# A graph layer's products of messages, each as two products on the two column halves of TensorE's array

## What is computed

```python
h  = silu(edge_scalars @ Wfc1 / 4)                 # per edge
w  = h @ Wfc2 / 8                                  # w0, w1, w2, w3
e0, e1 = f0[edge_src], f1[edge_src]                # gathered, turned features
mid0 = w0 * e0 * sh0;  mid1 = w3 * (e1 . sh1) / sqrt(3)
mid2 = w1 * e0 * sh1;  mid3 = w2 * e1 * sh0
n0..n3 = mean of mid0..mid3 over the edges of a destination node
alpha  = [n0, n1] @ Wa
conv   = [[n0, n1] @ Wl2_s, [n2, n3] @ Wl2_v]
out    = layernorm(x + sc + alpha * conv)
```

## Time and profile before

| | before |
|---|---|
| median of 3 timed runs | 932.54 us (929.51 to 934.15) |
| span of the profiled execution, first to last instruction | 930.5 us |
| TensorE busy | 880.9 us (95%) |
| VectorE busy | 812.1 us (87%) |
| GpSimd busy | 714.5 us (77%) |
| ScalarE busy | 632.5 us (68%) |
| products y on TensorE, L733 and L736 | 141.6 and 182.3 us |

### The profile page before, as it was taken

One profiled execution on the slowest core, in us unless ns is written; L12 is line 12 of the kernel. 1 busy time (PEld: TensorE's weight loads), 2 busy tenths in 40 slices (PEclk: granted clock), 3 DMA queues, 4 the chain that ended last, 5 costly groups with the idle time before them and its releaser, 6 DMA issues.

```text
span 930.5 us, 27956 instructions
## 1 busy us (share of the span) xinstructions
PE 880.9 (95%) x8336; PEld 758.5 (82%) x8336; DVE 812.1 (87%) x2797; ACT 632.5 (68%) x1961; POOL 714.5 (77%) x804
## 2 busy tenths in 40 slices
PE   3899999999999999999999889999999999999995
PEld 2778887888877878888888779989999898899994
DVE  3789999999988999999999978888888888888887
ACT  1555555555654555565565547888988888988887
POOL 6777777777777776777777318989998888989894
PEclk9999999999999999999999999999999999999998
DMA  6465554455565555456544227999999999999993
GB/s 181 118 178 159 163 143 127 133 140 131 140 133 133 168 156 150 132 160 181 153 131 133 86 84 231 305 305 302 303 302 301 300 304 295 300 306 308 304 298 136
DMA packets 87522, 186.47 MB, mean 200 GB/s; under 512 B 17647, under 2 KB 48139, under 8 KB 87372
## 3 DMA queue, kind: packets, MB, share of 16 engines
q1 hardware_dynamic: 48411, 87.72, 29.1%
q10 hardware_dynamic: 20016, 61.15, 19.7%
q0 software_dynamic: 18944, 35.81, 17.8%
HBM read 119.66 MB, written 64.95 MB: 198 GB/s over the span
## 4 chain that ended last, share of the span: by engine, by line
PE 46%; POOL 22%; issue 17%; DVE 11%; DMA 3%; ACT 1%; POOLq 0%; DVEq 0%; ACTq 0%
PE ps L795 7%; POOL res L640 7%; PE ps L736 7%; POOL gat L587 6%; PE ps L715 5%; POOL xa L628 5%; PE ps L733 4%; PE ps L805 4%; PE ps L696 4%; PE ps L702 4%; DVE mid L977 3%; PE ps L678 3%; POOL xa L624 3%; DVE z L995 2%; DMA gat<-spread,srcs 2%
## 5 line engine op out<-in xcount | busy, mean ns | idle before, releaser
L587 POOL DMA_INDIRECT gat<-turned,srcs x196 | 190.8, 973 | 66.6 <-issue 61.8
L587 POOL DMA_INDIRECT gat<-spread,srcs x196 | 188.7, 963 | 61.8 <-issue 60.0
L855 ACT ACTIVATE e_sb<-ps 128x512 f32<-128x512 f32 x196 | 106.4, 595 | 123.1 <-PE ps L702 122.0
L795 PE MATMUL ps<-win,hot 60*128 60x162 f32 x2352 | 189.1, 306 | 0.7 <-DVE hot L1318 0.7
L736 PE MATMUL ps<-wy,mid 128*128 128x161 f32 x784 | 182.3, 314 | 0.0
L795 PEld LDWEIGHTS ps<-win,hot 60*128 60x128 f32 x2352 | 164.9, 186 | 17.1 <-issue 16.5
L1001 DVE SCALAR_TENSOR_TENSOR msg<-ps,sha,z 128x161 f32<-128x161 f32 x392 | 151.0, 385 | 14.0
L640 POOL TENSOR_TENSOR res<-agg,pre 128x640 f32<-128x640 f32 x98 | 152.2, 1553 | 9.9 <-ACT agg L900 9.9
L733 PE MATMUL ps<-wy,mid 128*128 128x97 f32 x784 | 141.6, 262 | 0.2 <-DVE mid L977 0.2
L977 DVE TENSOR_TENSOR mid<-ps,e_sb 128x512 f32<-128x512 f32 x196 | 133.2, 680 | 2.2 <-PE ps L715 2.2
L878 ACT ACTIVATE fin<-res,shift,rstd 128x160 f32<-128x160 f32 x292 | 132.2, 539 | 1.3 <-DVE shift L1267 1.3
(11 more groups left out here) (104 smaller groups left out, 1543.2 us busy)
## 6 DMA issues: line engine op xcount, KB each, us to landing
win<-rows SPq DMA_DIRECT2D x392, 114.6 KB
rows<-msg SPq DMA_DIRECT2D x98, 326.0 KB
out<-fin ACTq DMA_DIRECT2D x47, 640.0 KB, 5.4
xin<-x_g ACTq DMA_DIRECT2D x92, 322.0 KB, 4.4
gat<-turned,srcs POOLq DMA_INDIRECT x196
gat<-spread,srcs POOLq DMA_INDIRECT x196
eas<-ea_t SPq DMA_DIRECT2D x7, 384.0 KB, 4.8
xin<-x_g SPq DMA_DIRECT2D x6, 322.0 KB, 4.2
```

What stands on the lines that cost most here:

```text
L587: pool.indirect_dma_start(out=gat[:, slot, first:first + of.shape[1]], out_offset=None, in_=of, in_offset=bass.IndirectOffsetOnAxis(ap=src ...
L795: last = nc.tensor.matmul(agg_ps[b1][:, 2 * h + k, 0:SW], hot[side(h), b1, k, c, :], win[side(h), (b - 1) % RING, k, c, 0:SW], start=c == ...
```

## The change

In `combine` each of the two products of a tile is made as two. The first loads the first 64 edges of `mid` and writes partitions 0 to 63 of y, the second loads the other 64 edges and writes partitions 64 to 127. All 128 rows of `mid` take part in each, and each streams the same columns of `wy` as before. `HALF` is 64. The semaphore is raised by the last of the four.

```diff
-                    nc.tensor.matmul(y[:, t, 0:W_Y1 - W_YA], mid[:, q % 2, t, 0, k, :],
-                                     wy[:, 0:W_Y1 - W_YA], start=True, stop=True)
                     of = (W_Y1, W_Y1B)[t] - W_YA
-                    nc.tensor.matmul(y[:, t, W_Y1 - W_YA:YW], mid[:, q % 2, t, 1, k, :],
-                                     wy[:, of:of + VEC + 1 + MUL0],
-                                     start=True, stop=True).then_inc(y_ready[t], 1)
+                    parts = ((0, 0, W_Y1 - W_YA, 0), (1, W_Y1 - W_YA, YW, of))
+                    for c, begin, end, w in parts:
+                        for n in range(2):
+
+                            edges = slice(n * HALF, (n + 1) * HALF)
+                            last = nc.tensor.matmul(y[edges, t, begin:end],
+                                                    mid[:, q % 2, t, c, k, edges],
+                                                    wy[:, w:w + end - begin],
+                                                    start=True, stop=True)
+                    last.then_inc(y_ready[t], 1)
```

## The result

| | before | after |
|---|---|---|
| median of the runs shared by one chip | 933.77 us (929.51 to 936.31, 10 runs) | 939.32 us (935.46 to 941.66, 10 runs) |
| span of the profiled execution | 930.5 us | 938.4 us |
| first and last L696 | 20.47 and 542.04 | 20.65 and 548.52 |

The changed kernel takes 1.0056 times as long (95% interval 1.0032 to 1.0079). It is slower, as forecast, by 5.5 us instead of 12: the direction held, and so did the prices of the change and of the loads, but the forecast was about twice what came.

What follows compares the result with a forecast made beforehand. It took an ordinary 5.22 us edge step as a loop through TensorE's first y, ScalarE and VectorE, TensorE having little to spare. Steps of 5.40 (+0.18 x 63, plus 0.7) add 12.0: 930.5 + 12.0 + 2.0 = 944.5 us, range 930 to 964.

Steps and rivals of the forecast that it cites:

- path A: TensorE alone in an ordinary step: +0.22 us less slack of 0 to 0.09 before L696, giving 5.35 to 5.44.
- Path C: Through the second transposes and ScalarE's L832, said to end before L696: a step of 5.30 to 5.41 us.
- The drain: TensorE drains at each change of array shape: 0.15 us each, three more a step, +0.45.
- The loads: Half-size weight loads of y no longer stick out: -0.06 us a product pair, -0.23 a step.
- The second rival: No drain between shapes that both have 128 rows: step 5.16 us, time 929; chance 0.14.
- the first rival: Weight loads of y gain nothing, a pair stays at 0.50 us: step some 5.62, time 963; chance 0.13.
- the third: Rival: y halves of 128 rows run one after the other, a pair takes 0.88 us, time 1101; chance 0.05.
- What the odd jobs of VectorE cover: In 17 edge-stage steps at 5.49 us TensorE waits for VectorE anyway, hiding the change; uncovered, another 3 us.
- The sum on TensorE: Per ordinary step, shape changes +0.45 us and weight loads -0.23, together +0.22 before slack.
- is paid in full: In an ordinary edge-stage step, any time added to TensorE was said to lengthen the step by as much.
- a faster one could give at most 0.2 a step: In the edge stage, speeding up TensorE gains at most 0.2 us a step, as GpSimd (5.0) and VectorE (4.99) set floors.
- the 12 steps at 5.34: Edge-stage steps between 5.26 and 5.42 us, mean 5.34, forecast to rise to 5.40, adding 0.7 us.

Runs made afterwards that it cites:

- E7: Kernel before with y in halves only for the second tile (t = 1) of both pairs, as many shape changes as the full change: 943.89 us, ratio 1.0106.
- E3: Kernel before plus one unread transposing product of 128 columns (0.11 us) between the last y and L696: 933.41 us, ratio 0.9992.
- E4: Kernel before plus three unread transposing products (0.33 us) between the last y and L696: 943.11 us, ratio 1.0111.
- E8: Changed kernel plus one transposing product of 128 columns (0.11 us) between the second transposes and second pair of y: 945.14 us, ratio 1.0124.
- E6: Changed kernel with all y in halves ahead of all transposes, ScalarE's copies reordered alike: 923.71 us, ratio 0.9913 to the kernel before.
- E5: Kernel before, whole products, with all four y ahead of all transposes, ScalarE's copies reordered alike: 930.15 us, ratio 0.9972.

## Why the direction was right and the size was not

The step of the prediction that failed is the slack of path A, what TensorE had to spare ahead of L696: it was put at 0 to 0.09 us and in effect at 0.04, and the runs measure 0.12. Path C, which held the choice up, was not there at all. The other terms of the sum held.

**The drain** held. L676 behind halves takes 0.26, as forecast, and a change of shape costs 0.15 on both sides (1.03 less two pairs at 0.44; 0.26 less 0.11); the steps alone give the same (E7). The timelines of the weight load of the second L676, first before, then after, show where it lies:

```profile
307.08 0.14 PEld L676 LDWEIGHTS ps<-ident,gat 128*128 128x128 f32 x1
```

```profile
308.62 0.14 PEld L676 LDWEIGHTS ps<-ident,gat 128*128 128x128 f32 x1 [0.23 <-issue]
```

Before, it follows the loads of y without a pause, while L736's two records (from 306.92, for 0.47) are under way; behind halves the loading stands idle for 0.23 first, with no wait that the profile shows. The second rival, that the array does not drain between shapes of 128 rows, falls with that row. The Trainium skill, in the section "Key Properties" of its page "TensorEngine Tiling (Array Packing)", says that a change of tiling mode drains TensorE. The runs agree, with 0.15 us a change, also where only the columns change.

**The loads** held. A product pair in halves takes 0.44 against 0.50 (E7), and the loads of L739 are 0.136 us at the median, where those of L733 were 0.190. The rows of loads of L739 (ns min/median/max, first and last start):

```profile
L739 PEld LDWEIGHTS ps<-wy,mid x3136: 132/136/140, 33.1 to 555.0; 128*64 128x64 f32 x196
```

With that the first rival falls, and with 16 records in 1.03 the third: one after the other they would take 1.76 and more. The records of the two halves start 7 ns apart.

**What the odd jobs of VectorE cover** held: 5.49 in the mean of those steps in both kernels.

**The slack of path A is the term that was mis-sized.** The sum on TensorE, +0.45 - 0.23 = +0.22, is what the rows give (+0.21). I allowed 0 to 0.09 for slack, from the distance between the last stream and the load of L696, and took 0.04 of it in effect: of 0.18 us between them I left at least half to the change of shape. In the changed kernel the last y begins at 406.71 and the load comes at 407.09, 0.38 later, where it was 0.48 (308.24 to 308.72), and the first product now starts with the load and not 0.03 behind it. E3 shows that at least 0.11 is free, E4 measures 0.12, and E8 that nothing of it is left in the changed kernel. In the rows of the result it is the 0.05 of "issue" in the chain of before, which I had not put into the sum, and the 0.07 by which L696 can start ahead of the modelled end of the last y when TensorE itself comes last. With the +0.23 that the steps give (5.33 against TensorE's own 5.10, E4) the sum closes: 5.22 + 0.23 - 0.12 = 5.33.

With it fell the sentence that a slower TensorE "is paid in full": 0.11 us a step cost nothing in E3. That a faster one could give at most 0.2 a step stood: E6 gave 0.19.

**Path C was no path.** I let it pull the choice up to 5.40, since it gave up to 5.41. It rested on L696 waiting for the copies of the step's own second transposes. `weigh(d - 1)` reads quad d - 1, and E5 shows the load of L696 ahead of those copies. The name t_sb beside the load in the timeline, which I had doubted for the message and then believed for path C, was wrong for both.

With +0.11 in place of +0.18 the forecast's own sum is 930.5 + 63 x 0.11 + 2.0 = 939.4 us; the 12 steps at 5.34 cover it. Measured: 939.3. That the two meet so closely is in part luck: the sum adds 6.9 us to 932.54, and the chip that ran both kernels shows 5.5 over 933.77 (3.0 to 7.4 by the interval).

## What to carry to other kernels

A change of the array's shape cost TensorE 0.15 to 0.19 us each time here, so smaller tiles paid only where the products of one shape stood together; count the changes of a step first, and try the order before the tile. An engine that seems to run without a gap can still have slack ahead of a product with several waits; one cheap dummy product there measures it, and the same dummy after an edit tells whether the slack is used up. Of two waits that end close together, the name that the trace gives is no proof: look up in the code from which step the operand is, and keep the distance to each candidate over several kinds of step.

## What the runs showed of the hardware that I had not expected

- The price of a change depends on what comes next: behind row halves 0.15 for a transpose, 0.19 for a whole y of 97 columns (E5), and 0.15 for a y in halves behind whole transposes.
- The first records of the two halves of a product start 7 ns apart, and two halves of 128 rows by 64 columns run side by side: a product pair takes 0.44 us so, 0.50 whole.
- The chain's row of L696 is 0.66 or 0.59 although the timeline shows the same product in both: the row starts at the modelled end of the one before it, so a shorter row can be an earlier start.
- The busy time of a line hides such a change: the loads' busy time fell by 37.8 us and TensorE's rose by 20.2, while the time rose by 5.5 (the spans of these two profiles by 7.9).
